# A decoder layer in a hand-ordered kernel: the second batch's column loads and projections placed among the first batch's maxima, and the second half of the first batch's piece splits given to GpSimd

## The reference, cut to what matters

```python
q = split_heads(x @ Wq + bq); k = split_heads(x @ Wk + bk); v = split_heads(x @ Wv + bv)
att = where(tril, einsum('bhqd,bhkd->bhqk', q, k) * scale, -inf)
y = einsum('bhqk,bhkd->bhqd', softmax(att), v)
x = layernorm(x + y @ Wo + bo)                               # self-attention
x = layernorm(x + cross_attention(x, ctx, mask))             # 64 keys
gate, up = silu(bitlinear(x, w_gate)), bitlinear(x, w_up)    # rounded weights and activations
x = layernorm(x + bitlinear(gate * up, w_down))
```

## Time and profile before

| | |
|---|---|
| median of 3 runs | 839.31 us (838.5 to 842.38) |
| the profiled execution | 839.25 us, of which the span is 837.2 us |
| PE | 785.0 us busy, 94% |
| DVE | 687.3 us busy, 82% |
| ACT | 575.8 us busy, 69% |
| GpSimd | 345.0 us busy, 41% |
| mean granted TensorE clock | 0.992 of full speed |
| DMA | 32.88 MB in 37188 packets, mean 39 GB/s |

### The profile page before, as it was taken

One profiled execution on the slowest core, in us unless ns is written; L12 is line 12 of the kernel. 1 busy time (PEld: TensorE's weight loads), 2 busy tenths in 40 slices (PEclk: granted clock), 3 DMA queues, 4 the chain that ended last, 5 costly groups with the idle time before them and its releaser, 6 DMA issues.

```text
span 837.2 us, 20734 instructions
## 1 busy us (share of the span) xinstructions
PE 785.0 (94%) x7712; PEld 387.7 (46%) x7738; DVE 687.3 (82%) x1261; ACT 575.8 (69%) x752; POOL 345.0 (41%) x582
## 2 busy tenths in 40 slices
PE   8799999999999999999999999999999998999996
PEld 6444355354553434534454343543545443445644
DVE  5999998768998799877999689884899848836698
ACT  3267965458866588655885679856697579864595
POOL 5742345314542345422544234454424404452344
PEclk9899999999999999999999999999999999999999
DMA  6542002200211000110130011020010000010001
GB/s 179 144 112 73 11 20 65 71 20 14 52 52 46 20 21 2 39 59 17 30 84 27 12 28 46 2 80 10 21 27 27 20 2 26 3 51 2 2 1 52
DMA packets 37188, 32.88 MB, mean 39 GB/s; under 512 B 9828, under 2 KB 33252, under 8 KB 37092
## 3 DMA queue, kind: packets, MB, share of 16 engines
q1 hardware_dynamic: 33844, 28.93, 12.3%
q0 software_dynamic: 1536, 1.58, 0.8%
q10 hardware_dynamic: 1712, 1.05, 0.5%
HBM read 14.55 MB, written 4.19 MB: 22 GB/s over the span
## 4 chain that ended last, share of the span: by engine, by line
PE 58%; DVE 26%; ACT 5%; issue 5%; POOL 3%; DMA 1%; SPq 1%; POOLq 0%; DVEq 0%; ACTq 0%
DVE shift L1410 12%; PE ps L1055 10%; PE ps L837 8%; PE ps L1040 6%; PE ps L1018 6%; PE ps L850 4%; PE ps L916 3%; PE ps L989 2%; PE ps L1001 2%; PE ps L801 2%; PE ps L946 2%; PE ps L958 2%; POOL xt L776 2%; DVE stats L1319 2%; PE ps L826 2%
## 5 line engine op out<-in xcount | busy, mean ns | idle before, releaser
L1410 DVE TENSOR_REDUCE shift<-ps 128x2 f32<-128x1024 f32 (+2 forms) x320 | 343.8, 1112 | 38.4 <-PE ps L1018 21.1
L1161 ACT ACTIVATE probs<-ps 128x1024 f32<-128x1024 f32 (+3 forms) x384 | 294.1, 811 | 113.0 <-PE ps L1040 110.3
L1055 PE MATMUL ps<-probs,v_aug 128*32 128x512 f32 (+3 forms) x1536 | 158.4, 500 | 0.3 <-ACT probs L1161 0.3
L716 POOL TENSOR_SCALAR_AFFINE_SELECT probs<-probs 128x512 f32<-128x512 f32 x128 | 81.4, 645 | 154.5 <-ACT probs L1161 153.7
L1018 PE MATMUL ps<-k_stack,q_stack 48*128 48x512 f16 (+3 forms) x768 | 115.6, 330 | 12.3 <-DVE shift L1410 6.3
L1040 PE MATMUL ps<-q_stack,k_stack 49*128 49x512 f16 (+3 forms) x768 | 115.0, 329 | 11.6 <-DVE shift L1410 4.2
L1040 PEld LDWEIGHTS ps<-q_stack,k_stack 49*128 49x128 f16 x768 | 37.8, 93 | 107.6 <-ACT probs L1161 35.5
L1018 PEld LDWEIGHTS ps<-k_stack,q_stack 48*128 48x128 f16 x768 | 41.3, 94 | 98.0 <-DVE shift L1410 34.5
L1102 ACT ACTIVATE full<-ps,bias_scaled,kq_scale 128x512 f32<-128x512 f32 x32 | 24.9, 779 | 42.2 <-PE ps L850 28.5
L1024 PE MATMUL ps<-causal,pick_h 64*128 64x64 bf16 x1024 | 53.2, 190 | 0.0
L1024 PEld LDWEIGHTS ps<-causal,pick_h 64*128 64x128 bf16 x1024 | 46.8, 96 | 13.2 <-issue 0.5
(11 more groups left out here) (238 smaller groups left out, 1371.2 us busy)
## 6 DMA issues: line engine op xcount, KB each, us to landing
q_stack<-part_sb SPq DMA_DIRECT2D x168, 32.0 KB, 2.0
k_stack<-part_sb SPq DMA_DIRECT2D x144, 32.0 KB, 2.0
xT<-in_x_cols SPq DMA_DIRECT2D x8, 512.0 KB, 4.8
xt<-in_x SPq DMA_DIRECT2D x8, 512.0 KB, 4.0
out_x<-xt SPq DMA_DIRECT2D x7, 512.0 KB, 3.0
q_stack<-shiftT SPq DMA_DIRECT2D x128, 1.0 KB
k_stack<-part_sb POOLq DMA_DIRECT2D x48, 32.0 KB, 2.0
region<-in_w_gate SPq DMA_DIRECT2D x4, 256.0 KB, 3.2
```

What stands on the lines that cost most here:

```text
L716: pool.affine_select(out=blk, in_=blk, compare_op=ALU.is_ge, fill=0.0, base=0, pattern=[[0, HG], [1, P]], channel_multiplier=-1).then_inc( ...
L1055: mm = pe.matmul(ps[DV * i:DV * (i + 1), SUM_BANK, off:BANK], v_aug[:, kb, at:at + DV], probs_of(b, n)[:, i, :], start=first, stop=last)
L1161: act.activation(probs_of(b, n)[:, 2 * p:2 * p + 2, :], pair(u)[:, :, 0:BANK - off], ACT.Exp, scale=exp_scale).then_inc(probs_ready, 1)
L1410: dve.tensor_reduce(to[:, :, pairs[0]:pairs[-1] + 1, qb % TH], pair(u)[:, :, 0:len(pairs) * w].rearrange("p j (h w) -> p j h w", w=w), AX. ...
```

## The change

Three things change together.

1. In batch 0 the splits of pieces 4 to 7 (`SLOTS` is 4) go to GpSimd whole, by the helper that later batches use. ACT and DVE keep the splits of pieces 0 to 3. The helper's wait for the low halves that DVE makes moves to the first split that GpSimd does.
2. `ORDER` is written anew. In batch 0 the projections of pieces 6 and 7 stand before the third group's first exponentials; both halves of batch 1's columns are loaded (`x`) among the first maxima (units 32 and 42 of the list instead of 57 and 130); batch 1's ranges are at 84 and 112 instead of 211 and 225, and its eight `kq` units at 117 to 254 instead of 247 to 417. The last maximum of batch 0 is unit 311 before and 314 now.
3. There are 55 `stir` units instead of 59. At the last maximum of batch 0, 26 had passed before and 22 now; near unit 430 it is 36 before and 32 now; the last 15 stand in the tail of batch 3 both times.

From about unit 430 on, the two lists have the same units in nearly the same places; a few stand some places earlier or later.

```diff
-STIRS = 59
+STIRS = 55
 ORDER = (
-    "rr6r0sr1sgr2sr3sr6r1wr0ggfgm23m01m45r6m01m23m45r6m01m23r4m01fffm56m23m01a45a23w6aa01w4a23am56m01om23m45w6ssa"
+    "rr6r0sr1sr2sr3sr6r1r0wr1gggfgm23m45m01m23m45m01r6m01m45m23sr6xm45m01m23r6m01w4a23sr5xm01a23aw4a56fm01fa23am4"
...
@@ split, on GpSimd
-                if (b, n) == (1, 0):
-                    pool.wait_ge(low_ready, NP)
+                if (b, n) == (0, SLOTS):
+                    pool.wait_ge(low_ready, SLOTS)
@@ GpSimd
-                if u.kind == "split" and u.b > 0:
+                if u.kind == "split" and (u.b > 0 or u.idx >= SLOTS):
                     split(u.b, u.idx)
@@ ACT
-                if u.kind == "split" and u.b == 0:
+                if u.kind == "split" and u.b == 0 and u.idx < SLOTS:
                     n = u.idx
-                    if n >= SLOTS:
-
-                        slot_left(act, 0, 0, n % SLOTS)
```

More of the change, by code:

```diff
@@ L86 @@
[L86 to L89 removed]
+    "rr6r0sr1sr2sr3sr6r1r0wr1gggfgm23m45m01m23m45m01r6m01m45m23sr6xm45m01m23r6m01w4a23sr5xm01a23aw4a56fm01fa23am4"
+    "5m01a23om45a23om01aa23a45am23ssa45m01ooom23a45am01z6z6m45gm23gm01rz6z6a45a23z6z6aa45a01w6aa45a23fz0z0afm23m4"
@@ new lines @@
+    "5o01oogoogr6om45a23a01r6rfffm45o01a23m45m23wa01r6rm45a01m23om45m01wfr6rm45a23fffgm01z6a45m23oa45m01a23om45m0"
+    "1wa23r6arm01a45ogm23a01aa45oa01am23w6a45a01aa45a01m23oom45m23m01wooa45r6a01m45go23oa45rm01a23om45a01m23r6rm0"
+    "1z4gz4m23m45wa01a23oa01m45z6aa23z6a01m45aa23om23a01aa45oa01m45aa23a01ar6m01a23a45om01aa23oom45a23om01rr6aa45"
+    "m23o01om45a23oaa23m01oa45am23z6z6m45a01om23oz6m01a45z6m23z6z6o01aweea45z6z6a01m45m23oaa01a45am01rom23m45a01o"
+    "oom23a01o45z6m23m01p45om23a45bp6a23m45a01p6ppa01a45a23om01m45a23m01z6m45m23op01m45z6m23m01p6m23m01ba45p6pp4p"
@@ new lines @@
+    "5p0p1paa23oa45ap6a23p0p1p4a56aa23oa01aa23a56p4op13m56oz0a56p23p05p23z4z4z4p23p01m23a45z6p01p23a45m01oom23m45"
+    "p01z6z6m23m01m45p6o23p0a45oa23a01pm45z6m23ogga01pm45a23apopa01m45a23papr6m23a45a01aoa45a23am01p45oa23m01m45p"
+    "6om01p2p3p4m01m56p2p3p4p0p2p3pa45r6m23xaa01oogopppp6a01ao45z2p6pa23a45aoa23m01pppp45p6p2r3a01aa45a01ppppp23p"
+    "6m45m01z6z6p6p4aa23a01oaa56a23oaooppm01m45r6a01ppp23m45a01p6p23m45aa01p6p2ppp01a45o23oom45a01m23p6m01m23m45o"
+    "xoop6pa23a45o01oa23oa45pm23a01oa45m23a01z6p45m23m01m23m45p6m23m01m45p6paoa01p6p2p3p4pa01aa56op2a01am56a34a01"
@@ new lines @@
+    "atp2p3p4a01a56om23a01p4oora23p04r6r2rp01p24r6p01op23p45o01ogp45a01p23om01cp23ez6m45m01a23p6m01m23a45p6pa01m4"
+    "5a23oz6a01m23paom45a01z6m23a01z6m45aa01a23aorgga45a01aa23ppm45a01ppooaa45m23m01r6m23a45m01arp23m45om01oa23p6"
+    "o45m23om01p4p6p5m23p4m01m56p2p4p3p0p2a45r6paa23m01pppp4p5pa23aa01oa23m45roapooa01bpm23r6o45pp23p0p6pa45raa23"
+    "a01oaa23a45am01gpm23ppp45p6p0p1pa45a23oooopppp45m01m23p6o01om45p23p6a01m45ga23p6ppa01p4p5p6p01m23op4m23a01a5"
+    "6p4ppa23a01a56ar4m01m23a56om01a45aa23om45m01p23om45m23p6m45m01p2pp6ra45ap3p0a12ga45p6paa23m45a01op6p2p3a01m4"
@@ new lines @@
+    "5oooa01a23p6o45a01p6om45p02m45r6p01p25tp01op01m23p45m01a23p45p01a23m45m01p23m45rom23m01p6p4pa01a23aa56r4pm23"
+    "m01a56aoem23a45a01oapa23a01aa45rm23a01ppoaom45m01a23r6pa45m23p01oom45m23m01p6gr4m23m01p6p4p5p2p6m34m01p5p2p3"
+    "p4o56aa01pooa45aa23a01pppp6p4paxa23a01apppr5p23p4p6opooa45m01a23r6pppo23m01p45p6xap2p3a01a45ogaa01a23aa45pa0"
+    "1m23om45om23pppbp01p6m45p01m23p6p0ppp23om01m45a23p6a01om23p4a23o01a56oa01a23pm45pom01a23a45oaa01ra23om45p01m"
+    "23m45m01p6m45m23m01p6pap4p5p2p3a01oa01pam45oga01p6p3a01aa45p2p6a01m45ta23p6ooom01r4p25co01r4p23p04p23rr6rgp0"
@@ L90 @@
+    "vvhu3u6u5hhh01h4h6uuuz2v45hhhhh23h6h0h1v6uu4u0z5v5v4v6z0hhhuv5hh01v4h6uuuh01u23vvvvv4v6vh5h0hu23u6u4uvvvv23h"
+    "z5z5v23v5v4vtuvtt"
 )
```

53 lines of the change are left out of this document (15 added, 38 removed).

## The result

| | before | after |
|---|---|---|
| median of 15 runs each on one chip | 838.61 us (837.71 to 842.38) | 842.89 us (840.77 to 844.6) |
| ratio, 95% interval | | 1.0048 (1.0039 to 1.0056) |
| the profiled execution | 839.25 us, span 837.2 us | 844.14 us, span 842.4 us |

The kernel is 0.5% slower, 4.3 us by the medians. I had forecast 836.7 us, 2.6 us less. The profiled execution of after lies 1.25 us above its median and that of before 0.64 us above its own, so of the 5.2 us between the spans about 0.6 are chance.

A forecast was written before the change was run, and what follows sets the result against it. DVE was taken to bound batch 0's maxima, PE alone 150 to 200 us, the layer norm and quantisation chain the end. Terms -2.1 - 2.8 - 0.7 + 1.5 + 2.0 - 0.5 = -2.6 gave 836.7 us, range 830.5 to 844.5.

The forecast's parts named there:

- those 8 us come back in the stretch in which PE alone is the bound: Four batch 1 projections moved ahead of batch 0's last maximum return their PE time behind it, from 150 to 200 us.
- The cost of the early projections: Four more projections less four stirs put 5.9 us more PE work before batch 0's last maximum, delaying it up to that.
- Filled gaps, -2.8: At the start, a value projection (-1.6) and piece 6's projection (-1.2) move into PE's idle time; bounds 0 and -2.8 us.
- Splits behind the masks, +1.5 (bounds 0.5 and 3): Near 40 us, evictions of pieces 6 and 7 wait for GpSimd's splits, delaying first exponentials and PE: +1.5 us.
- the slower rival: PE starves at the late first exponentials and behind the moves, its clock falling each time: 846 us, chance 0.15.
- no gain: Rival: every us moved forward opens as a wait, 840.2 us; band 839.5 to 843, chance 0.18.
- Moves in ACT's queue, +2.0: From about 55 to 60 us, ACT issues six q moves ahead of exponentials PE needs: +2.0 us, bounds 0 and 4.
- Stirs, -2.1: Four fewer stirs by batch 0's last maximum save PE 2.1 us, if nothing idles in their place.
- DVE relief, -0.7: DVE loses four low halves of pieces 4 to 7, about 3.0 us; worth -0.7 us, bounds 0 and -3.0.
- DMAs, -0.5: 48 of SP's 96 batch 1 move issues come before batch 0's last maxima instead of behind: -0.5 us, 0 to -1.6.
- The port rule: GpSimd's four moved subtracts block DVE's small steps 1.16 us each: 841.3 us if all catch one, 837.9 with two half catches.

## Why the prediction was wrong

**The step that failed** is "those 8 us come back in the stretch in which PE alone is the bound". I read it from PE at 48.4 of 50 us and DVE's idle 8 us. Four stirs and four projections made PE look full there (in all, stirs are 6.8 us and projections 7.9 us of the stage's 99.7); without ten stirs the stage kept its length. 0.7 us came back in it, 1.7 us to the end. My sum had PE 2.1 us less busy and 0.5 us less idle; it was 1.8 us busier and 3.4 us more idle, and 2.8 us of that idle time is in this stage. DVE's 8.0 us of idle did go, but turned into 2.8 and 4.4 us elsewhere in the stretch.

**The cost of the early projections** I had right in kind: 5.9 us of PE work more, by projections less stirs. By the trace it is 8.0 - 3.3 = 4.7, and PE is busy 5.6 in all, of which 1.3 is the chance in the warm-up matmuls. The place came 6.9 us later against 2 to 6 forecast (6.0 in the other trace with the same list up to there).

**Filled gaps, -2.8**: the gaps did fill, and no time came of it. Up to the end of the second group (36.7 us before, 37.4 after) PE is idle 3.2 us instead of 6.6. But DVE runs without a gap up to 37 us in both kernels (from 22.6 us before, from 23.2 after), so the group ends no earlier; I had named DVE as the bound of these maxima and then booked PE's gap as a gain. What PE had filled was paid at once: a value projection of 2.0 us took 3.08 at 27.05, at half speed behind waits of 0.19, 0.20, 0.73 and 0.41 us, and in the third group PE is idle 5.5 us instead of 1.3. For pieces 6 and 7 I named the bank as the risk; it was the split ahead of them.

**Splits behind the masks, +1.5 (bounds 0.5 and 3)**: right in mechanism, low in size. Behind the masks' end (37.37, forecast 36.75) the first split came only after 2.3 us of drain, which the code shows and I left out. PE waited 3.5 us and DVE 3.2, past the upper bound; putting the splits back is worth 2.3 us by the ratios. A half-speed stretch came behind it, as the slower rival had it, and that rival also has the sign; the time, 842.9 us, lies in the band of "no gain" (839.5 to 843), at its upper end.

**Moves in ACT's queue, +2.0**: PE's wait there is 0.56 us, and it is for DVE. DVE takes maxima without a gap from 52.0 to 60.6 us and `tops` from 61.2, so it and not ACT sets the pace; the lower bound, 0, is nearer.

**Stirs, -2.1, DVE relief, -0.7, DMAs, -0.5**: the stirs went, DVE's total fell by 2.2 us, and none of it is in the time. Leaving out more stirs gave nothing or lost. DVE waits 14.4 us for PE between 22 us and the last maximum, 4.4 before, so I take its relief to be worth nothing; no run tests it or the DMAs' term alone in the new order.

**The port rule**: the Trainium skill, SBUF — State Buffer, section "Who interferes with whom", has a DVE instruction with two SBUF inputs contend with a GpSimd instruction that reads SBUF. The traces agree in kind: L1416 took 0.41 us at 137.31 where GpSimd's add L722 ran until 137.68, and 0.18 in after at the same step. But moving four splits onto GpSimd in the old order changed DVE's small steps (L1416 and L1417) by 0.2 us in all, and the time by 0.1%. By that rule the sum would have been 1.2 to 4.6 us worse; such meetings were rare here.

**Open**: why about 2 us of the new order's loss (the last maximum at 141.2 us with the splits back, 839.25 us before and 841.9 with them) can be taken out neither by fewer stirs nor by an earlier start. The runs don't separate the amount of early work from its place: whatever took work away ahead of the last maximum also lowered the clock, but for one version (12 stirs for four projections, 1.6 us less), whose last maximum came 1.5 us earlier, 0.7 of it there by 30 us by chance. Which single neighbour makes the loss was not found.

## What to carry to other kernels

An engine that is 97% busy is not thereby the bound: filler work, and real work that lies in a chain's waits, look the same in a busy share. Take out filler there and see whether the stretch gets shorter before you book a gain from it; here it kept its 99.7 us within 0.2, and adding cost the whole length added. In a kernel whose engines never overtake their own queue, price a moved unit with everything that it drags along on the other queues (splits, moves, evictions) and with what stands behind each of them: a 1.8 us split ahead of `apply` held it for 4.7 us, 2.7 of them in the split's own wait for its piece.

## What the runs showed of the hardware

- A drain behind a few GpSimd operations took 2.2 us (2.31 us of idle with it, 0.1 without), more than the split behind it.
- The clock fell to half speed behind rather short waits: without 14 stirs the granted clock is 0.57 from 130 to 135 us, where no wait of PE was longer than 1.0 us.
- A step of DVE stood beside a memset of GpSimd until it had ended, in both traces. The step, on 128x16, takes 0.26 us on average; this one took 0.77, to 29.96, and the memset ran to 29.92. In after it took 0.90, to 30.59, and the memset ran to 30.55. DVE and GpSimd, kernel before:

```profile
29.19 0.77 DVE L1417 TENSOR_SCALAR shift_h<-shift 128x16 f16<-128x16 f32 x1
...
28.95 0.97 POOL L665 MEMSET off_pick<- 80x1024 bf16 x1
```

```profile
L1417 DVE TENSOR_SCALAR shift_h<-shift 128x16 f16<-128x16 f32 x32 | 8.3, 260 | 1.1
```
